# Expert routing on quarters of the array, four output buffers, and a feed-forward pass laid over a butterfly product

## The chip, the core and the metric

The kernel runs on one core of a Trainium2 chip. The core has five engines that are used here: TensorE (PE, matrix products from SBUF into PSUM), VectorE (DVE), ScalarE (ACT), GpSimd (POOL) and SyncE (SP, which here only issues DMA transfers); POOL issues transfers too. Engines order themselves by semaphores: an instruction adds to one when it ends, another engine waits until it has reached a number. Each engine works through its own instructions in the order in which they are written. The metric is the device time of one execution in microseconds (us), the median of several runs.

## The reference

Two layers work on x of 2 x 2048 tokens with 256 features, in float32. Each layer is a mixer (a state space scan) followed by a feed-forward block, with layer norms around them. The change is in the feed-forward block of layer 0 and in the end of layer 1.

Layer 0's block is a mixture of experts with 64 slots. Tokens stand in groups of 16. In each group every slot takes the token with the highest logit:

```python
logits = einsum('...btd,des->...btes', grouped, controller) + tie
perm = (logits == max(logits, axis=-3))
sel = einsum('...btd,...btes->...besd', grouped, perm)
inner = relu(einsum('...besd,desf->...besf', sel, f1) + bias)
inter = einsum('...besf,esfd->...besd', inner, f2)
out = einsum('...besd,...btes->...btd', inter, perm)
```

So there is one 256 x 64 matrix f1 and one 64 x 256 matrix f2 for each of the 64 slots.

The end of layer 1 has two parts that add into one output. The first takes y, the sum of both directions of the mixer: f = relu(W1.y + b1) with 512 hidden features, then y + W2.f + b2, a layer norm over features, and the residual x1 is added. The second takes the normed input xn: a matrix W_exp (256 to 1024), ten butterfly stages over the 1024 features, a bias, gelu, ten more butterfly stages and a matrix W_con back to 256. A butterfly stage mixes each feature with the one whose index differs in one bit, by 2 x 2 weights. The kernel folds the butterfly stages into the two matrices, once, and then multiplies tokens by the folded matrices.

## The kernel before, in words

P is 128, C is 2 (halves of 256 features), TT is 512 tokens, T is 4096 tokens, HB is 8 (blocks of 128 in 1024), FB is 4 (blocks of 128 in 512). `banks` are PSUM tiles of 512 float32 columns; there are eight. A float32 matmul or its weight load appears as two records in the trace, a transpose as one. The name in a trace row is stage_tile: exa is the routing and the expert products, fly the butterflies, fin and finb the last stage.

**experts0.** For each of the two batches, four quarters of 512 tokens are routed, and then eight expert groups (of eight slots) are multiplied. Routing of a quarter: PE computes the logits (line 949) and turns the tokens around with an identity matrix (line 956); DVE adds the tie term, takes the maximum over each group, compares and multiplies by a parity mask (lines 906 to 913), which gives pq; PE transposes pq (line 960); ACT keeps pq in perm_t (862) and the turned tokens in work (864). Two groups of 16 tokens share 32 partitions. To select rows, DVE spreads each transposed 128 x 128 piece into pex, four copies of which three quarters are zero (918, with pair_of as mask), and PE multiplies with all 128 rows and 512 columns (969), eight times a quarter. ACT copies each result into sel_t with the axes turned (870): consecutive elements go to addresses 512 bytes apart. One quarter ends before the next one starts.

For a group of slots, PE forms the first products (979, two column tiles of 64 at a time, `first_products`), DVE adds the bias and applies relu (927, 931), PE forms the second products (993, two row tiles of 64 at a time, `second_products`), and ACT and DVE copy half each into one of two output buffers `inter` (880, 935). POOL stores a buffer (846), waits for the store (850) and then posts slot_free, for which the copies wait. SP loads f1 and f2 of a group into two buffers each (831, 834).

**butterflies and last.** `butterflies` folds ten stages into `up` and `down`, [128, 8, 257] each. Three of them, the cross-block stages, mix whole blocks: ACT scales a block (1906) and DVE adds the scaled partner (1917), eight blocks a stage; then DVE copies the result back (1921). The other seven, the lane stages, mix partitions within a block. For each of 7 x 8 steps and each of the two matrices DVE builds a 128 x 128 matrix with two nonzeros in a row (1950, 1956), PE multiplies a block by it (1973) and ACT copies the result back (1987). `down` gets its cross-block stages first, `up` last. Then the block of instructions ends, and a second one begins. There PE transposes `up` (2064), and for each of eight tiles of 512 tokens it runs hidden (2073), feed (2080), half of upward (2088), mean (2101), the rest of upward, variance (2107) and downward (2112). ACT applies relu, gelu, square, log and exp, DVE the residual (2157), the centring (2163), three Newton instructions (2166 to 2172), scale, shift, x1 and the final sum (2188). The next tile's first matmul waits for the end of the sum. SP loads y and x1 of a tile, POOL stores the output (2053).

## Time and profile before

| | |
|---|---|
| median of 3 runs | 3668.19 us (3656.0 to 3673.11) |
| the profiled execution | 3672.47 us, its span 3670.8 us |
| experts0, routing and products | 680 to 937 us of the span |
| last, both parts | 3181.5 to 3670.8 us of the span |
| PE busy | 2889.5 us (79%) |
| DVE busy | 2834.1 us (77%) |
| ACT busy | 1881.2 us (51%) |
| POOL busy | 2287.1 us (62%) |
| granted TensorE clock, mean | 0.916 |

The span runs from the first to the last instruction of one profiled execution. Busy shares are averages over stages with different limits; the two mixers lie between and before the stages of the change. A granted clock of 1.00 is 2.4 GHz, 0.50 is 1.2 GHz.

### The profile page before, as it was taken

The page shows a single profiled execution, that of the slowest core. Times are in us where ns is not written, and L with a number is a line of the kernel's source. Part 1 is how long each engine was busy: PE and PEld are TensorE (multiplying, and loading weights), DVE is VectorE, ACT ScalarE, POOL GpSimd, SP SyncE. Part 2 cuts the span into 40 slices and gives each one's busy share as a digit, 9 for nine tenths or more (in the row PEclk, how much of TensorE's full clock was granted, in tenths as well). Part 3 has the DMA queues.
Part 4 walks back from the last instruction along what each step waited for, and adds up shares of the span by engine and source line. Part 5 has one row for each costly group of instructions (what it writes and reads, how often), then busy time and mean ns, then how long its engine had stood idle before and what let it go on. Part 6 is the DMA issues. An engine that isn't in the chain of part 4 may idle for free. (4 is left out here: it accounts for less than half of the span.)

```text
span 3670.8 us, 27563 instructions
## 1 busy us (share of the span) xinstructions
PE 2889.5 (79%) x7494; PEld 1196.8 (33%) x7494; DVE 2834.1 (77%) x2237; ACT 1881.2 (51%) x2469; POOL 2287.1 (62%) x1102
## 2 busy tenths in 40 slices
PE   5677677767556879788898888798897887579998
PEld 2222222344222333333333333233333332244443
DVE  4899799433238999999999999999999999462222
ACT  4575576434245555555555655555555554352222
POOL 2598399100116989889889899898899898100000
PEclk7799699899777999999989999999899999889999
DMA  1011011153714444554555455555445555201110
GB/s 58 16 51 47 7 52 50 35 183 114 245 52 153 158 172 172 166 183 168 168 179 172 157 182 177 165 172 174 169 162 181 179 178 200 83 23 34 34 34 11
DMA packets 163606, 451.10 MB, mean 123 GB/s; under 512 B 23328, under 2 KB 52192, under 8 KB 163456
## 3 DMA queue, kind: packets, MB, share of 16 engines
q1 hardware_dynamic: 156576, 424.60, 34.5%
q0 software_dynamic: 6912, 25.17, 1.7%
q8 instruction: 45, 0.74, 0.1%
q14 instruction: 73, 0.60, 0.1%
HBM read 414.85 MB, written 34.87 MB: 123 GB/s over the span
## 5 line engine op out<-in xcount | busy, mean ns | idle before, releaser
L1317 POOL TENSOR_TENSOR mix_prod<-mix_spread,mix_h 128x1024 f32<-128x1024 f32 x512 | 1374.4, 2686 | 247.4 <-DVE mix_h L1723 131.4
L1817 PE MATMUL mix_banks<-mix_prod,kept_ident 128*128 128x512 f32 x2048 | 1049.6, 638 | 80.9 <-POOL mix_prod L1317 54.1
L1367 ACT ACTIVATE mix_side_in<-mix_dt,mix_neg_a 128x1024 f32<-128x1024 f32 x384 | 437.7, 1141 | 315.6 <-DVE mix_h L1723 312.2
L1817 PEld LDWEIGHTS mix_banks<-mix_prod,kept_ident 128*128 128x128 f32 x2048 | 406.1, 202 | 515.8 <-issue 302.9
L1709 DVE TENSOR_TENSOR mix_banks<-mix_banks,mix_dtu 128x1024 f32<-128x1024 f32 x384 | 467.1, 1216 | 10.0 <-PE mix_banks L1807 5.9
L1723 DVE TENSOR_TENSOR_SCAN mix_h<-mix_side_in,mix_state,mix_banks 128x1024 f32<-128x1024 f32 x192 | 450.6, 2347 | 18.1 <-issue 0.4
L1807 PE MATMUL mix_banks<-mix_parts,kept_sel 96*128 96x512 bf16 x768 | 250.0, 410 | 260.5 <-DVE mix_h L1723 252.4
L1723 DVE TENSOR_TENSOR_SCAN mix_h<-mix_side_in,mix_banks 128x1024 f32<-128x1024 f32 x192 | 438.8, 2286 | 18.9 <-ACT mix_side_in L1367 1.3
L1327 POOL TENSOR_TENSOR mix_side_in<-mix_spread,mix_dtu 128x512 f32<-128x512 f32 x256 | 339.0, 1324 | 0.1
L2053 POOL DMA_DIRECT2D out<-finb_o x8 | 5.8, 728 | 525.0 <-DVE finb_eps L2192 525.0
L435 POOL TENSOR_TENSOR mix_drive<-mix_drive,mix_du 128x1024 f32<-128x1024 f32 x128 | 305.2, 2400 | 40.5 <-ACT mix_drive L500 40.3
L638 DVE TENSOR_TENSOR_SCAN mix_h<-mix_banks,mix_state,mix_drive 128x1024 f32<-128x1024 f32 x128 | 296.2, 2339 | 23.7 <-POOL mix_drive L435 21.4
L1359 ACT ACTIVATE mix_state<-mix_h 128x1 f32<-128x1 f32 x256 | 51.7, 202 | 412.4 <-DVE mix_h L1723 411.6
L1807 PEld LDWEIGHTS mix_banks<-mix_parts,kept_sel 96*128 96x128 bf16 x768 | 60.1, 101 | 557.0 <-DVE mix_h L1723 449.4
L1367 ACT ACTIVATE mix_banks<-mix_dt,mix_neg_a 128x1024 f32<-128x1024 f32 x128 | 141.9, 1109 | 121.7 <-DVE mix_h L1723 121.2
L740 PE MATMUL mix_banks<-mix_prod,kept_ident 128*128 128x512 f32 x352 | 178.4, 631 | 10.7 <-DVE mix_u L656 10.7
L846 POOL DMA_DIRECT2D slot_outputs<-exa_inter x32 | 18.3, 573 | 258.1 <-DVE exa_inter L935 181.6
L506 ACT ACTIVATE mix_banks<-mix_dt,mix_neg_a 128x1024 f32<-128x1024 f32 x128 | 141.5, 1105 | 44.4 <-DVE mix_h L638 44.1
L1723 DVE TENSOR_TENSOR_SCAN mix_h<-mix_banks,mix_state,mix_side_in 128x1024 f32<-128x1024 f32 x64 | 149.3, 2333 | 0.0
L1723 DVE TENSOR_TENSOR_SCAN mix_h<-mix_banks,mix_side_in 128x1024 f32<-128x1024 f32 x64 | 145.4, 2272 | 0.0
L500 ACT ACTIVATE mix_drive<-mix_dd,mix_mask 128x1024 f32<-128x1024 f32 x128 | 145.1, 1133 | 0.0
L1579 DVE SCALAR_TENSOR_TENSOR mix_u<-mix_x,mix_taps,mix_u 128x1024 f32<-128x1024 f32 x96 | 122.6, 1279 | 16.1 <-ACT mix_u L1396 15.8
(264 smaller groups left out, 4499.4 us busy)
## 6 DMA issues: line engine op xcount, KB each, us to landing
mix_spread<-c_rows SPq DMA_DIRECT2D x640, 512.0 KB, 3.9
mix_c_row<-c_rows SPq DMA_DIRECT2D x40, 512.0 KB, 3.6
exa_f<-f SPq DMA_DIRECT2D x32, 512.0 KB, 4.8
slot_outputs<-exa_inter POOLq DMA_DIRECT2D x32, 512.0 KB, 3.9
ln_zp<-slot_outputs SPq DMA_DIRECT2D x8, 2048.0 KB, 10.2
first_acc<-xT SPq DMA_DIRECT2D x8, 512.0 KB, 4.1
x_scratch<-first_acc POOLq DMA_DIRECT2D x8, 512.0 KB, 4.0
fw_scratch<-mix_res SPq DMA_DIRECT2D x8, 512.0 KB, 6.3
```

Source lines behind the costliest of these rows:

```text
L435: pool.tensor_tensor(r.drive[:, i % 3, :], r.drive[:, i % 3, :], part(du, i // NS), ALU.add).then_inc(r.drive_ready, 1)
L500: act.activation(r.drive[:, i % 3, :], part(dd, i // NS), ACT.Copy, scale=mask[:, at:at + 1]).then_inc(mask_ready, 1)
L506: act.activation(decay[i % 2], part(dt, i // NS), ACT.Exp, scale=neg_a[:, at:at + 1]).then_inc(r.decay_ready, 1)
L638: dve.tensor_tensor_scan(r.h[:, i % 3, :], decay[i % 2], r.drive[:, i % 3, :], state[:, at:at + 1], ALU.mult, ALU.add).then_inc(r.scan_don ...
L740: mm = pe.matmul(y_bank[:, q, :], which, r.prod[:, i % 2, q * TT:(q + 1) * TT], start=i % NS == 0, stop=True, skip_group_check=True)
L1317: pool.tensor_tensor(prod[:, un % 2, :], spread[:, i % SLOTS, :], h[:, un % HR, :], ALU.mult).then_inc(prod_ready, 1)
L1327: ins = pool.tensor_tensor(half(side_in[:, 2, :], hf), half(spread[:, i % SLOTS, :], hf), half(dtu[:, g % MB, :], hf), ALU.mult)
L1367: act.activation(drive[un % 2] if pooled(un) else side_in[:, un % 2, :], dt[:, at // NS, :], ACT.Exp, scale=neg_a[:, way(p), at:at + 1]).t ...
L1709: dve.tensor_tensor(drive[un % 2], drive[un % 2], dtu[:, at // NS, :], ALU.mult).then_inc(drive_ready, 1)
L1723: dve.tensor_tensor_scan(h[:, un % HR, step], a_in[:, step], b_in[:, step], state[:, at:at + 1] if p % NC else 0.0, ALU.mult, ALU.add).the ...
L1807: mm = pe.matmul(half(drive[un % 2], hf), k.sel[:, at % NS, :], half(parts[:, p % 2, :], hf), start=True, stop=True)
L1817: mm = pe.matmul(y_bank[:, hf, :], k.ident[:], half(prod[:, un % 2, :], hf), start=False, stop=True, skip_group_check=True)
```

## The change

In experts0:

- Selecting no longer uses pex and pair_of. A transposed pq is copied once into pq_t, and for every 128 tokens and each half of the features four matmuls with 32 rows each (partitions 0 to 31, 32 to 63 and so on) and 128 columns are issued, each with its own PSUM bank, 4 to 7. A quarter is done in two halves of two 128-token pieces. ACT copies banks 4 and 5 of a half, DVE banks 6 and 7, each by four instructions of 256 elements.
- The tokens are transposed straight from xn; work has two halves for the turned tokens.
- The logits of the next quarter are issued ahead of the selecting matmuls of this one, and DVE makes the next quarter's choice ahead of its copies.
- There are four output buffers in place of two. ACT and DVE wait for the store itself instead of slot_free. DVE's relu of the next group stands ahead of its copies of this group.
- All loops are written out instead of run by registers.

In last, the two blocks of instructions are one. W1 and y of tile 0 are loaded first. The parts hidden, feed, mean and variance of all eight tiles, with their norm and residual, are run first, results in `base` (all eight tiles stay in SBUF). The lane steps are spread over tiles 1 to 5: each tile has eight places, and SLOT_STEPS says how many steps it gets. Each direction has one PSUM bank in place of two. The results of the cross-block stages are used where they are, without the copy back. Mean, centring, square, variance and root of a tile are done during the next tile, the finish during the one after it. `across(1)` stands on ACT behind tile 0's relus, `across(0)` ahead of tile 7's relus. Then `up` is transposed over two banks, with the rest of tile 7's norm in between, and eight tiles of upward, gelu and downward follow with nothing else than the final sum. SP stores the output.

The core of the diff, its new lines (the old ones stand in the functions above). First experts0: POOL, the copies that two engines share, DVE, selecting, and the order on PE:

```diff
+                for n in range(B * NE):
+                    b, e = n // NE, n % NE
+                    for h in range(2):
+                        r = (2 * n + h) % KEPT
+                        pool.wait_ge(act_kept, 2 * n + h + 1)
+                        pool.wait_ge(dve_kept, 2 * n + h + 1)
+                        pool.dma_start(z[b, :, e * EG + h * 4:e * EG + h * 4 + 4, :], inter[:, r]).then_inc(stored[r], 16)
+                for r in range(KEPT):
+                    pool.wait_ge(stored[r], 16 * (2 * B * NE // KEPT))
+
+            def selected(i, hh, v, c):
+
+                t0 = i % NQ * QG + hh * 16
+                to = sel_t[:, c, :, t0:t0 + 16].rearrange("p s (t g) -> p t g s", t=2)[:, :, 2 * v:2 * v + 2, :]
+                return to, banks[:, 4 + v, :].rearrange("p (t c g s) -> p t c g s", t=2, c=C, g=2)[:, :, c]
...
+                def keep_turned(i):
+                    dve.wait_ge(turned, i + 1)
+                    if i >= 2:
+                        dve.wait_ge(sel_ready, 2 * (i - 1))
+                    dve.tensor_copy(pq_t[:, i % 2].rearrange("p t n -> p (t n)"), banks[:, 3, :]).then_inc(pq_ready, 1)
+
+                def keep_selected(i, hh):
+                    dve.wait_ge(sel_ready, 2 * i + hh + 1)
+                    if i // NQ:
+                        dve.wait_ge(in_ready, i // NQ * NE)
+                    for v in (2, 3):
+                        for c in range(C):
+                            to, of = selected(i, hh, v, c)
+                            ins = dve.tensor_copy(to, of)
+                    ins.then_inc(dve_sel, 1)
...
+                def select(i, hh):
+                    b, j = i // NQ, i % 2
+                    pe.wait_ge(xtok_ready, i + 1)
+                    pe.wait_ge(pq_ready, i + 1)
+                    if i or hh:
+                        pe.wait_ge(act_sel, 2 * i + hh)
+                        pe.wait_ge(dve_sel, 2 * i + hh)
+                    if b and i % NQ == 0 and hh == 0:
+                        pe.wait_ge(inner_ready, b * NE)
+                        pe.wait_ge(act_kept, b * 2 * NE)
+                        pe.wait_ge(dve_kept, b * 2 * NE)
+                    for t in range(2):
+                        for c in range(C):
+                            for v in range(4):
+                                rows = slice(32 * v, 32 * v + 32)
+                                o = (t * C + c) * P
+                                mm = pe.matmul(banks[:, 4 + v, o:o + P], xtok[rows, j, 2 * hh + t, c * P:(c + 1) * P],
+                                               pq_t[rows, j, 2 * hh + t, :], start=True, stop=True)
+                    mm.then_inc(sel_ready, 1)
...
+                for b in range(B):
+                    logits(b * NQ)
+                    turn(b * NQ)
+                    for i in range(b * NQ, (b + 1) * NQ):
+                        ahead = i + 1 < (b + 1) * NQ
+                        if ahead:
+                            logits(i + 1)
+                        for hh in range(2):
+                            select(i, hh)
+                        if ahead:
+                            turn(i + 1)
+                    pe.wait_ge(act_sel, 2 * NQ * (b + 1))
+                    pe.wait_ge(dve_sel, 2 * NQ * (b + 1))
+                    first_products(b * NE)
                     for e in range(NE):
                         if e + 1 < NE:
-                            first_products(e + 1)
-                        second_products(e)
+                            first_products(b * NE + e + 1)
+                        second_products(b * NE + e)
```

Then last: loads, the order on ACT, finish, the order on DVE, the lane steps and the order on PE:

```diff
+            def load_y(i):
+                if i >= 2:
+                    sp.wait_ge(summed, i - 1)
+                sp.dma_start(y[:, i % 2], token_tile(k.y, i, L)).then_inc(y_loaded[i % 2], 16)
+
+            def load_x1(i):
+                if i >= 2:
+                    sp.wait_ge(finished, i - 1)
+                sp.dma_start(x1[:, i % 2], token_tile(k.x1, i, 0)).then_inc(x1_loaded[i % 2], 16)
+
+            sp.dma_start(w1[:], a["W1"].rearrange("(c p) m -> p c m", p=P)).then_inc(w1_loaded, 16)
+            load_y(0)
+            for dst, src in ((b1[:], a["b1"]), (vec[:], a["vec"]), (up_b[:], a["up_bias"])):
+                sp.dma_start(dst, src).then_inc(vec_loaded, 16)
+            sp.dma_start(fac[:], a["factors"]).then_inc(fac_loaded, 16)
+            sp.dma_start(down[:, :, 0:E], a["W_con"].rearrange("(j p) e -> p j e", p=P)).then_inc(down_loaded, 16)
+            sp.dma_start(w2[:], a["W2"].rearrange("(c p) m -> p c m", p=P)).then_inc(w2_loaded, 16)
+            load_y(1)
+            sp.dma_start(up[:], a["exp"].rearrange("(j p) e -> p j e", p=P)).then_inc(up_loaded, 16)
+            load_x1(0)
+            load_x1(1)
...
+            act.preload_act_table_set("natural_log_exp_and_others")
+            act.wait_ge(vec_loaded, 48)
+            act.wait_ge(filled, 1)
+            for i in range(NT):
+                if i == NT - 1:
+                    across(0)
+                at = marks(i)
+                for h in range(FB):
+                    relu(i, h)
+                    lanes(at[h], at[h + 1])
+                if i == 0:
+                    act.wait_ge(fac_loaded, 16)
+                    act.wait_ge(down_loaded, 16)
+                    across(1)
+                lanes(at[4], at[5])
+                if i:
+                    square(i - 1)
+                lanes(at[5], at[7])
+                if i:
+                    root(i - 1)
+                lanes(at[7], at[8])
+            square(NT - 1)
...
+            def finish(i):
+                dve.wait_ge(root_ready, i + 1)
+                dve.scalar_tensor_tensor(out=ra[:], in0=banks[:, 7, :], scalar=EPS, in1=r0[:], op0=ALU.add,
+                                         op1=ALU.mult).then_inc(newton, 1)
+                dve.wait_ge(newton, 5 * i + 1)
+                dve.scalar_tensor_tensor(out=ra[:], in0=ra[:], scalar=-0.5, in1=r0[:], op0=ALU.mult,
+                                         op1=ALU.mult).then_inc(newton, 1)
+                dve.wait_ge(newton, 5 * i + 2)
...
+            for i in range(NT):
+                at = marks(i)
+                lanes(at[0], at[1])
+                if i >= 2:
+                    finish(i - 2)
+                lanes(at[1], at[4])
+                if i:
+                    centre(i - 1)
+                lanes(at[4], at[7])
+                residual(i)
+                lanes(at[7], at[8])
+                if i == NT - 2:
+                    across(0)
+            dve.wait_ge(crossed[0], ACROSS * HB)
+            dve.tensor_tensor(up_b[:], up_b[:], spare[:, :, E:W].rearrange("p j o -> p (j o)"), ALU.add).then_inc(biased, 1)
...
                     for w in range(2):
-                        i = n * (2 * HB) + (2 * j + w)
-                        slot = (2 * j + w) % 4
-                        pe.wait_ge(mat_ready, i + 1)
-                        pe.wait_ge(kept, i + 1)
-                        pe.matmul(banks[:, slot, 0:width], mat[:, slot, :], way[w][0][:, j, :], start=True,
+                        if s == 0:
+                            pe.wait_ge(up_loaded, 16)
+                            pe.wait_ge(crossed[1], ACROSS * HB)
+                        pe.wait_ge(mat_ready, 2 * s + w + 1)
+                        if s:
+                            pe.wait_ge(kept, 2 * (s - 1) + w + 1)
+                        src = spare if w and n == 0 else way[w][0]
+                        pe.matmul(banks[:, w, 0:W], mat[:, (2 * s + w) % 4, :], src[:, j, :], start=True,
                                   stop=True).then_inc(turned, 1)
 
...
+            for i in range(NT):
+                at = marks(i)
+                for h in range(FB):
+                    hidden(i, h)
+                    lanes(at[h], at[h + 1])
+                if i:
+                    mean(i - 1)
+                lanes(at[4], at[5])
+                for c in range(C):
+                    feed(i, c)
+                    lanes(at[5 + c], at[6 + c])
+                if i:
+                    variance(i - 1)
+                lanes(at[7], at[8])
+            pe.wait_ge(crossed[0], ACROSS * HB)
+            for n in range(HB * C):
+                if n >= 2:
+                    pe.wait_ge(w_ready, n - 1)
+                else:
+                    pe.wait_ge(kept, 2 * len(lane_steps))
```

## Rows read from the trace of the kernel before

**Rows 1.** Busy time by stage: stretch, length, busy us of each engine, PEclk, DMA share, GB/s.

```profile
680.00:940.00 260.00, 178.18 (x1024) 100.90 (x1024) 84.28 (x131) 103.02 (x121) 18.33 (x32) 0.87 0.36 130
3181.50:3670.80 489.30, 424.02 (x1072) 199.49 (x1072) 159.56 (x436) 167.58 (x296) 5.83 (x8) 0.95 0.10 33
```

**Rows 2.** The same view inside the experts stage: routing, products, twice, and two groups.

```profile
681.90:753.10 71.20, 55.06 (x128) 21.31 (x128) 21.73 (x32) 42.04 (x44) 0.00 (x0) 0.85 0.08 28
753.10:811.00 57.90, 37.85 (x385) 31.54 (x385) 19.69 (x32) 9.74 (x17) 8.10 (x14) 0.88 0.75 264
811.00:879.40 68.40, 51.50 (x130) 19.79 (x130) 21.73 (x32) 41.45 (x44) 1.06 (x2) 0.90 0.06 22
879.40:937.00 57.60, 33.77 (x384) 28.27 (x384) 19.68 (x32) 9.55 (x16) 9.16 (x16) 0.89 0.70 255
786.00:798.00 12.00, 7.79 (x96) 6.70 (x96) 4.76 (x8) 2.39 (x4) 2.21 (x4) 1.00 0.87 308
```

**Rows 3.** Order of events, one quarter of the routing: start us, duration us, instruction.

```profile
810.89 0.30 PEld L949 LDWEIGHTS exa_banks<-kept_xn,exa_ctrl 128*128 128x128 f32 x2 [2.41 <-issue]
...
815.09 0.69 DVE L913 TENSOR_TENSOR exa_pq<-exa_lt,exa_parity 128x512 f32<-128x512 f32 x1
...
826.50 0.30 PEld L949 LDWEIGHTS exa_banks<-kept_xn,exa_ctrl 128*128 128x128 f32 x2 [0.59 <-issue]
```

**Rows 4.** Groups by form in the experts stage.

```profile
L870 ACT ACTIVATE exa_sel_t<-exa_banks 128x512 f32 x64 | 63.7, 1040 | 28.4 <-PE exa_banks L969 28.3
...
L935 DVE COPY exa_inter<-exa_banks 128x512 f32<-128x512 f32 x32 | 22.1, 691 | 65.6 <-POOLq L850 50.6 <-PE exa_banks L993 15.0
...
L880 ACT ACTIVATE exa_inter<-exa_banks 128x512 f32<-128x512 f32 x32 | 19.1, 597 | 91.2 <-POOLq L850 70.7 <-PE exa_banks L993 20.5
```

**Rows 5.** Busy time by stretch in the last stage; the last is one tile.

```profile
3181.50:3201.70 20.20, 0.00 (x0) 0.00 (x0) 13.27 (x44) 9.92 (x24) 0.00 (x0) 0.50 0.53 165
3201.70:3259.10 57.40, 56.65 (x224) 39.17 (x224) 54.36 (x222) 43.19 (x113) 0.00 (x0) 0.97 0.00 0
3259.10:3282.10 23.00, 3.67 (x16) 2.91 (x16) 14.76 (x44) 9.89 (x24) 0.00 (x0) 0.66 0.18 61
3332.10:3379.80 47.70, 45.17 (x104) 19.55 (x104) 9.65 (x16) 13.07 (x17) 0.75 (x1) 1.00 0.11 33
```

**Rows 6.** Order of events: matmuls on tiles of the array, and the last output copy.

```profile
756.79 2.00 PE L993 MATMUL exa_banks<-exa_f,exa_work 64*128 64x256 f32 x16
...
787.98 1.97 PE L979 MATMUL exa_banks<-exa_sel_t,exa_f 128*64 128x128 f32 x32
...
794.11 1.97 PE L979 MATMUL exa_banks<-exa_sel_t,exa_f 128*64 128x128 f32 x32
...
931.21 0.69 DVE L935 COPY exa_inter<-exa_banks 128x512 f32<-128x512 f32 x1 [0.69 <-POOLq L850]
...
952.78 0.64 PE L1042 MATMUL ln_by_token<-ln_zp,exp_perm_t 128*32 128x256 f32 x8
```

**Rows 7.** Order of events in the last stage.

```profile
3187.95 3.31 ACT L1906 ACTIVATE fina_spare<-fin_down,fina_fac 128x257 f32<-128x257 f32 x8 [18.90 <-DMA fin_down<-W_con]
...
3199.71 1.23 DVE L1921 COPY fin_down<-fina_spare 128x2056 f32<-128x2056 f32 x1
...
3276.64 0.39 SPq L2042 DMA_DIRECT2D finb_y<-both_scratch  x1
...
3282.12 9.47 PE L2073 MATMUL finb_banks<-finb_y,fin_w 128*128 128x512 f32 x16 [6.15 <-DMA finb_x<-x_scratch]
...
3316.51 13.90 PE L2112 MATMUL finb_banks<-finb_g,fin_down 128*128 128x512 f32 x32
...
3332.13 7.13 PE L2073 MATMUL finb_banks<-finb_y,fin_w 128*128 128x512 f32 x16 [1.72 <-DVE finb_eps L2192]
```

**Rows 8.** Groups by form in the last stage.

```profile
L1987 ACT ACTIVATE fin_up<-fly_banks 128x257 f32<-128x257 f32 x56 | 21.6, 386 | 13.5 <-PE fly_banks L1973 7.9
...
L2166 DVE SCALAR_TENSOR_TENSOR finb_ra<-finb_banks,finb_r 128x512 f32<-128x512 f32 x8 | 5.5, 691 | 71.2 <-ACT finb_r L2138 71.2
```

815 lines of the change are left out of this document (384 added, 431 removed).

## The prediction

> **What bounds the kernel now.** I read the busy shares by stage first. The two touched stages hold 260 us (experts) and 489.3 us (last) of the 3670.8 us [rows 1]; nothing between them is edited, so only these count.
>
> The experts stage runs a routing part and a product part for each batch [rows 2]. In routing PE is 77% busy and nothing is full. The order of events shows a strict chain per quarter of 512 tokens: logits from 810.89, DVE's choice until 815.8, two kinds of transposes, then eight selecting matmuls that wait for ACT's copies, and the next logits at 826.50: 15.6 us [rows 3]. ACT pays for the copies: 1040 ns to scatter 512 elements into sel_t, against 597 ns for 512 written in long runs [rows 4]. The products are held by the round output copy, store, slot free: ACT and DVE wait 70.7 and 50.6 us for POOL's slots [rows 4], and the DMA engines are 70 to 87% busy [rows 2].
>
> The last stage has four pieces in a row: 20.2 us of loads and the first cross-block steps, 57.4 us of butterflies, 23.0 us of cross-block steps, transposes and loads, then eight tiles of 47.7 us, in which PE works 45.2 [rows 5]. PE's own work sets nearly all of the tiles.
>
> **The experts, routing.** Removed: ACT's copy of the tokens, pair_of, pex and DVE's four products into it per quarter, and eight full-size matmuls (16 records of 0.43 us, 6.9 us). Added: 32 matmuls of 32 rows and 128 columns (64 records); eight copies of 256 elements on ACT and eight on DVE; one DVE copy of 512 (pq_t).
>
> The new shape of matmul is in no row. Four column tiles took 0.64 us for eight records of 256 columns; two row tiles took 2.00 us for 16 such records, 0.108 us apart after the first; two column tiles of 128 columns took 1.97 us for 32, 0.055 apart [rows 6]. If four row tiles run side by side, a record costs about 0.04 us, 2.6 us a quarter; if each weight load has to follow the last, 0.108 us, 6.9 us, as now. I take 0.04, since tiles overlap in all three rows, and keep 0.108 as the bound. The Trainium skill ("TensorE: Matmul & The Clock Gate", LDWEIGHTS (loading the stationary operand)) speaks against this change: a load goes by columns, 32 rows costing as much as 128; one after another that gives the second value. Its Part 3 has loads of different row groups overlap, which gives the first.
>
> Copies: ACT needs 386 ns for a dense 257 [rows 8] and 597 for 512 [rows 4], a fixed part of 0.17; with it the scattered 1040 gives 0.60 us for a scattered 256, 2.5 us with handover for a half's four. DVE's dense copy of 512 takes 691 ns [rows 4]; its scattered 256 is in no row. Bounds 0.35 (half of it) and 0.60 (ACT's); I take 0.60, the nearest scattered row. The Trainium skill ("SBUF — State Buffer", Door 1: The DMA port swizzle) says that accesses which leave a 16-byte line each time pay; ACT's two rows agree (1040 against 597), and by it DVE pays too.
>
> A quarter then, from the moment turned(i) is posted: DVE copies pq_t while PE does the logits of i+1 (to 1.8), chooses for i+1 (4 x 0.72, to 4.7), copies half 0 (2.4, to 7.2). Only then may PE select half 1, as banks 4 to 7 are single: behind that wait on PE stand the transposes of i+1. Select and latencies 1.5, DVE's copies 2.4, to 11.1, and the next keep_turned follows. DVE's cycle is 0.7 + 2.9 + 2.4 + 1.5 + 2.4 + 0.4 = 10.3 us; ACT's, 9 us, hides behind it. PE is half busy in it, and the granted clock was 0.85 and 0.90 with more [rows 2]; at 1.2 GHz logits and select(1) cost 2.9 more. I take 11. A batch: first logits, choice and transposes 5.6, three quarters 33, the last, with nothing to choose, 9.7: 48.3 us. Before: 71.2 and 68.4 [rows 2]. **Gain 43 us.** Bounds: 9 us a quarter (gain 56), 14 (gain 24).
>
> **The experts, products.** Four output buffers end the slot round, and DVE's relu goes ahead of the copies. What is late next is the DMA: a group moves 1 MB in and 1 MB out, and the engines were 0.87 busy at 308 GB/s [rows 2], so 354 GB/s when full: 5.9 us for 2.1 MB. Undisturbed groups already take 6.1 us (787.98 to 794.11 [rows 6]). PE needs 2.0 + 2.0 us, DVE 2.6. SP issues f1(n+1) behind f2(n), which waits for second_products(n-2): as before. The parts take 57.5 and 52.5 us now to the last copy (931.9 [rows 6]); 6.6 for the first group and 7 x 6.1 make 49.3 after. **Gain 11 us**; bounds 27 (5.0 us a group: PE's 4.0 and its handovers) and a loss of 1 (7.0). Setup: PE waits for the tie load, which lands when the removed memsets end: nothing. Loops written out: no row prices fetching the longer code; taken as nothing, bound 2 us either way.
>
> **Last stage, start.** PE's first matmul is at 3201.76 now [rows 5]. After, W1 and y(0) are first in SP's queue, 1 MB together; two such loads now hold PE from the issue at 3276.64 until 3282.12, 5.5 us [rows 7], so PE starts near 3187. Its first 16 records run cold as at 3282 (9.47 us against 7.13 [rows 7]), relu 0.9, feed 6.9: 3204.1. Factors and W_con come behind the small vectors, in time, for ACT starts across(1) only behind relu(0,3), at 3197.2: 11.7 us (3187.95 to 3199.7 [rows 7]), then residual(0) 1.4 on DVE, then the first matrix: PE resumes at 3211.1, after 5.3 us idle. The two copies of 1.23 us behind the cross-block steps are gone.
>
> **Tiles 1 to 5 over the butterflies.** PE work of a tile: 40 records (16 hidden, 16 feed, 8 mean and variance) of 0.4292 (13.90 us for 32 [rows 7]) are 17.2 us; 11 steps of four records of half that, 9.5: together 26.7. The stalls, walked through in DVE's order:
> - centre(i-1) stands ahead of the matrices that PE wants right behind mean(i-1): 0.2 + 1.3 + 0.7 = 2.25 us.
> - finish(i-2), seven instructions x 0.72 = 5.0 [rows 8], stands ahead of slot 1: 0.6; residual 1.4 ahead of slot 7, with ACT's root between its two copies: 0.9.
> - one bank per direction: the second step of a slot waits for ACT's 0.39 us copy [rows 8]: 0.3 to 0.5, three times, 1.2.
> That is 31.6 us a tile. Tile 1 (no finish, 12 steps) ends at 3236.3, tile 5 at 3362.7, the steps behind it at 3368.3.
>
> **Tiles 6 and 7, transition.** Tile 6: 17.2, to 3385.5. In tile 7 across(0) stands ahead of all relus on ACT and begins behind root(5): 1.6 + 11.2 + 0.7, PE idle 10.1 us and then cold (3.4 us more); variance(6) ends at 3416.3. Transposes go over two banks instead of four, 0.33 us each instead of 0.22 (3.67 us for 16 [rows 5]), with finish(6) (1.6 + 5.0), mean(7) 1.7, centre(7) 1.3 and variance(7) 1.7 in line: 16.7 us and 2.3 cold: 3435.3.
>
> **Final tiles.** 64 records x 0.4292 = 27.5 us x 8 = 219.8: 3655.1; two additions 1.3 and a store from SP 4.2: 3660.6 against 3670.8. So the eight tiles shrink by 162 us, and the part ahead of them grows from 100.6 to 253.8 us, by 153: PE does the same matmuls. **Gain 10; I take 8**, since PE may be cold behind the 5.3 us too. Bounds: all stalls of the tiles gone (25 us) and tile 7's wait halved, gain 38; twice the stalls, loss 17.
>
> **Sum.** 43 + 11 + 8 = 62 us. The profiled execution took 3672.5 (span 3670.8), so 3610.5; the median 3668.2 lies 4.3 lower, so **3606 us**.
>
> **Rivals.**
> - *Row tiles do not overlap.* Each half's select takes 3.4 us instead of 1.3; both lie mostly on the cycle, with more cold clock: 14 us a quarter, gain 24, sum 43: 3625. For it: the overlapping rows have 64 rows or narrow weights; against: they all overlap. 0.17.
> - *The last stage hides its stalls:* gain 38 there: 3576. For it: DVE has only 18 us of work in a 31.6 us tile. 0.15.
> - *The four buffers do nothing,* as the DMA keeps the products at their time: 3617. 0.12.
> - *The other side: PE falls to 1.2 GHz in the interleaved part.* 137 + 48 = 185 us of PE work lie between 3187 and 3435 and double when cold; once 43% of it is cold (80 us = 62 + 18) the kernel is slower by over 0.5%; all of it: 3791. Against: gaps of 1.7 us between today's tiles leave the clock at 1.00, and the butterflies run at 0.97 [rows 5, 7]. 0.04.
> - The forecast: 0.52.
>
> **How the numbers follow.** The range goes from the well hidden last stage with a little more from the routing (3570) to the serial row tiles with a loss in the last stage (3640). Under 0.5% (18 us) a change of this kernel can't be told from none. Faster takes all cases but the cold one and the far end of the bounds: 0.92; same 0.04; slower 0.04.
>
> **What would show it.** Right: selecting records some 0.04 us apart; 10 to 12 us between logits; no waits for POOL, and DMA share near 0.9 in the products; PE's first matmul of the last stage 5.5 us behind its first load; about 31 us a tile, with PE waiting for matrices behind mean; 27.5 us a final tile. Wrong: weight loads of 0.1 us in a row; scattered DVE copies far from 0.6 us; PEclk under 0.9 in the interleaved part; a wait in tile 7 that isn't 10 us.

## The result and the profile after

The changed kernel takes 3600.8 us (median of 4 runs, 3594.44 to 3601.67) against 3667.24 (median of 4, 3656.0 to 3673.11): a ratio of 0.9826, 95% interval 0.9804 to 0.9848, so 56 to 72 us less. The forecast was 3606 us, 62 us less by its sum. The profiled execution took 3600.97 us, with a span of 3599.2.

First the stretches of the changed kernel, in the view of busy time by stretch (its columns are those of [rows 2] and [rows 5]): routing, products, routing, products; the whole last stage; and in it the start, tiles 1 to 5, tile 6 with the wait of tile 7, the rest of tile 7 with the transposes, and the eight final tiles.

```profile
680.50:730.60 50.10, 31.16 (x320) 22.21 (x321) 28.65 (x52) 21.20 (x40) 0.00 (x0) 0.77 0.11 37
730.60:781.30 50.70, 38.03 (x384) 32.09 (x385) 19.58 (x32) 9.56 (x16) 8.20 (x15) 0.84 0.78 280
781.30:829.50 48.20, 30.23 (x320) 22.18 (x320) 28.65 (x52) 21.21 (x40) 0.53 (x1) 0.78 0.14 56
829.50:878.30 48.80, 36.53 (x384) 30.92 (x384) 19.46 (x33) 9.58 (x17) 7.98 (x15) 0.88 0.76 271
3121.20:3599.20 478.00, 428.66 (x1072) 204.31 (x1072) 149.26 (x411) 145.16 (x282) 0.00 (x0) 0.96 0.10 34
3126.70:3150.70 24.00, 18.36 (x37) 7.66 (x37) 12.24 (x32) 13.13 (x29) 0.00 (x0) 0.86 0.49 169
3150.70:3312.90 162.20, 144.84 (x421) 80.07 (x422) 87.10 (x272) 62.90 (x145) 0.00 (x0) 0.96 0.09 30
3312.90:3343.00 30.10, 20.60 (x48) 8.77 (x47) 15.91 (x34) 15.90 (x34) 0.00 (x0) 0.89 0.10 35
3343.00:3374.90 31.90, 25.05 (x57) 11.14 (x58) 17.32 (x37) 5.38 (x7) 0.00 (x0) 0.84 0.05 17
3374.90:3594.70 219.80, 219.80 (x513) 96.68 (x511) 13.84 (x21) 46.57 (x67) 0.00 (x0) 1.00 0.05 17
```

Set against [rows 2] the reader sees where the time went: routing took 71.2 and 68.4 us and takes 50.1 and 48.2; the products went from 57.9 and 52.5 (to the last copy, [rows 6]) to 50.7 and 48.8. From the first logits to the last output copy that is 250.0 us before and 197.8 after: 52.2 less. The first logits come 1.4 us earlier. The last stage took 489.2 us from its first load to the end of the span and takes 477.8, 11.4 less. Both stages differ by some us between profiles of one program; how much is said with the first and the second experiment. These make 65.0 of the 71.6 us between the two spans. The other 6.6 lie between the last output copy and the last stage, where no line is changed; run before_again below says what they are.

One quarter of the new routing, in the order of events (start us, duration us, instruction, and in brackets the idle time ahead of it and what ended it):

```profile
788.72 0.69 DVE L922 COPY exa_pq_t<-exa_banks 128x512 f32<-128x512 f32 x1 [0.75 <-PE exa_banks L996]
...
790.33 1.17 PE L1015 MATMUL exa_banks<-exa_pq_t,exa_work 32*128 32x128 f32 x32
790.44 0.69 DVE L905 TENSOR_TENSOR exa_lt<-exa_banks,exa_tie 128x512 f32<-128x512 f32 x1 [1.03 <-PE exa_banks L978]
...
793.22 1.86 DVE L931 COPY exa_sel_t<-exa_banks 128x256 f32<-128x256 f32 x4
...
795.23 2.09 PE L1015 MATMUL exa_banks<-exa_pq_t,exa_work 32*128 32x128 f32 x32 [3.73 <-DVE exa_sel_t L931]
...
797.38 1.92 DVE L931 COPY exa_sel_t<-exa_banks 128x256 f32<-128x256 f32 x4 [2.29 <-PE exa_banks L1015]
...
800.11 0.69 DVE L922 COPY exa_pq_t<-exa_banks 128x512 f32<-128x512 f32 x1 [0.81 <-PE exa_banks L996]
```

The 32 records of one selecting half take 1.17 us at 2.4 GHz, 0.037 us apart, and 2.09 at 1.2 GHz. From one copy of pq_t to the next go 11.4 us: DVE works for 7.2 of them and waits 4.1 for PE. PE in turn waits 3.73 us for DVE between the two halves, because the whole choice for the next quarter stands ahead of DVE's copies; behind that wait it runs at 1.2 GHz.

The groups by form of the same stage:

```profile
L1027 PE MATMUL exa_banks<-exa_sel_t,exa_f 128*64 128x128 f32 x512 | 42.3, 337 | 24.0 <-DMA exa_f<-f 20.0 <-ACT exa_sel_t L869 4.1
...
L869 ACT ACTIVATE exa_sel_t<-exa_banks 128x256 f32<-128x256 f32 x64 | 30.7, 630 | 41.1 <-PE exa_banks L1015 41.1
L931 DVE COPY exa_sel_t<-exa_banks 128x256 f32<-128x256 f32 x64 | 30.2, 585 | 20.1 <-PE exa_banks L1015 20.1
...
L952 DVE COPY exa_inter<-exa_banks 128x512 f32<-128x512 f32 x32 | 22.1, 690 | 8.2 <-PE exa_banks L1042 4.1 <-DMA slot_outputs<-exa_inter 4.0
```

A scattered copy of 256 elements takes 630 ns on ACT and 585 on DVE. The output copies wait 4.0 us in all for a store, where they waited 50.6 and more for POOL [rows 4]; PE's wait is now the load of f1, 20.0 us.

In the last stage, one tile over the butterflies, and the wait in tile 7:

```profile
3228.94 1.88 PE L2231 MATMUL fin_banks<-fin_base,kept_mean 128*128 128x512 f32 x4
3230.86 1.28 DVE L2130 TENSOR_TENSOR fin_base<-fin_base,fin_banks 128x512 f32<-128x512 f32 x2 [4.87 <-PE fin_banks L2231]
...
3232.85 0.70 PE L2253 MATMUL fin_banks<-fin_up,fin_mat 128*128 128x257 f32 x2 [2.03 <-DVE fin_mat L2114]
...
3249.05 0.67 PE L2253 MATMUL fin_banks<-fin_up,fin_mat 128*128 128x257 f32 x2 [0.94 <-DVE fin_mat L2114]
...
3343.05 2.93 PE L2211 MATMUL fin_banks<-fin_y,fin_w 128*128 128x512 f32 x3 [9.55 <-ACT fin_f L2043]
```

DVE's centring (1.28 us) stands between mean and the next matrices, and PE waits 2.03 us for them. Behind that wait feed's first eight records run partly at 1.2 GHz in this tile and in tile 1 (5.29 and 5.02 us, where others take 3.60):

```profile
3202.45 3.60 PE L2222 MATMUL fin_banks<-fin_f,fin_w 128*128 128x512 f32 x8
...
3233.82 5.29 PE L2222 MATMUL fin_banks<-fin_f,fin_w 128*128 128x512 f32 x8
```

The first is tile 2, the second tile 3. At the end of each tile PE waits another 0.94 us, and in tile 7 9.55 us for the relu behind across(0). From one tile's first hidden record to the next it is 31.4, 33.1, 31.4 and 31.4 us for tiles 2 to 5. Tile 1 takes 33.0 from the second of its four hidden products on; the first stands ahead of the butterflies.

### The profile page after: what moved, and what is told of

Same layout as the page of the kernel before. It is cut to its first block and busy times, and to the rows that moved or that the text cites. A ratio compares the mean times of both kernels' runs of the same rounds, so it can differ in the third digit from the quotient of the medians.

```text
span 3599.2 us, 26475 instructions
## 1 busy us (share of the span) xinstructions
PE 2852.6 (79%) x7878; PEld 1208.1 (34%) x7878; DVE 2831.8 (79%) x2234; ACT 1817.9 (51%) x2447; POOL 2280.4 (63%) x1094
## 5 line engine op out<-in xcount | busy, mean ns | idle before, releaser
L435 POOL TENSOR_TENSOR mix_drive<-mix_drive,mix_du 128x1024 f32<-128x1024 f32 x128 | 305.2, 2400 | 41.2 <-ACT mix_drive L500 40.8
L2199 DVE TENSOR_TENSOR fin_base<-fin_banks,fin_base 128x512 f32<-128x512 f32 x16 | 10.3, 686 | 204.4 <-PE fin_banks L2271 204.4
L838 POOL DMA_DIRECT2D slot_outputs<-exa_inter x32 | 17.2, 539 | 205.7 <-DVE exa_inter L952 201.3
```

The source lines that it names most:

```text
L435: pool.tensor_tensor(r.drive[:, i % 3, :], r.drive[:, i % 3, :], part(du, i // NS), ALU.add).then_inc(r.drive_ready, 1)
```

## The experiments

Times are medians; a ratio is that to the kernel before, run beside it on the same chip, with its interval. Stage times are from each run's own profile. "The changed kernel" has 197.8 us in the experts stage (from the start of the first logits to the end of the last output copy; the expectations have 197.9) and 224.1 from the first butterfly matmul (3150.69) to the first upward matmul (3374.79). The interval of the changed kernel (0.9804 to 0.9848) overlaps those of all the kernels below that try to improve on it, except all_tuned; what each of them gains is read from stage times, of one profile each.

### Each half alone: experts_only, last_only

```diff
 # experts_only: kernel before, with
-def experts0 of before
+def experts0 of the changed kernel
 # last_only: changed kernel, with experts0 of before
```

> The kernel before with the new experts stage alone; the last stage is the old one. My theory: the two halves of the change do not touch each other, so the experts stage keeps its 197.8 us from the first logits to the last output copy (250.0 before) and the last stage its 489 us. That is 52 us, a time near 3615. The changed kernel's profile also has 6.3 us less inside the unedited second mixer (first to last POOL product there 2006.7 us against 2013.0) and 1.4 us less ahead of the first logits. Theory A: the 6.3 us are a difference between two executions, so this run shows a mixer anywhere between 2005 and 2015 us, unrelated to the edit. Theory B: they come from the new experts stage (its code or its buffers move what follows), so the mixer takes 2007 us here and 2013 us in the run with the last stage alone.

> The changed kernel with the experts stage of before, so the new last stage alone. My theory: the last stage takes 478 us against 489.2, a gain of 11, a time near 3656. The rival that says the last stage is worth nothing gives 3667, and that it hides its stalls 3629. The tiles must show the same pieces as in the changed kernel: 24.0 us from the first matmul to the first butterfly matmul, some 32 us a tile, 9.6 us of wait in tile 7, 27.5 us a final tile. For the mixer between the stages: 2013 us if theory B of the run beside this one holds, any value from 2005 to 2015 if theory A does.

experts_only: 3606.45 us, ratio 0.9853 (0.9831 to 0.9875), 46 to 62 us. Its experts stage takes 197.8 us. last_only: 3655.48 us, ratio 0.9977 (0.9964 to 0.9989), 4 to 13 us. Its pieces are those of the changed kernel: 23.8 us to the first butterfly matmul, 163.8 for tiles 1 to 5, 9.6 of wait in tile 7. So the halves add up, and each is worth about what was forecast (54 and 8). The old experts stage takes 256.5 us in last_only's profile and 250.0 in the first one: the old stage itself varies, the new one stays within 0.5 us in the six profiles that hold it unchanged.

The new last stage varies too. Six profiles hold it unchanged: in three (the changed kernel, two_buffers, split_choice) it takes 477.7 to 477.8 us from its first load to the end, in three (last_only, rows_in_turn, three_loads) 482.8 to 483.0; from the first butterfly to the first upward matmul that is 224.0 to 224.1 and 228.6. The waits are the same, and the 4.5 us are records at 1.2 GHz: 1.6 in tiles 1 to 5, 2.9 behind them. The clearest is variance(7), in the changed kernel and in rows_in_turn:

```profile
3373.06 1.89 PE L2239 MATMUL fin_banks<-fin_sq,kept_mean 128*128 128x512 f32 x4
```

```profile
3404.96 3.62 PE L2239 MATMUL fin_banks<-fin_sq,kept_mean 128*128 128x512 f32 x4
```

The old last stage took 489.1 to 489.8 us in its three profiles, so the new one gains 6 to 12 us and not 11.4 each time, which fits last_only's 4 to 13. The second mixer took 2003.6 us in experts_only and 2013.0 in last_only; that alone would fit theory B.

### The mixer that nobody edited: before_again

> The kernel before, profiled once more. The unedited second mixer took 2013.0 us from its first to its last POOL product in both profiles with the old experts stage, and 1996.3 to 2007.0 in eight with the new one; the granted clock in it was 0.94 in the long ones and 0.96 in the two of 1996.3. If its length is set by the execution and its clock, this profile may show any value in 1996 to 2015; if the new experts stage shortens it, 2013 again.

The mixer from its first to its last POOL product, by stretch: before, before_again, and a kernel with the new experts stage (two_buffers):

```profile
1114.10:3127.10 2013.00, 1685.29 (x3904) 669.63 (x3904) 1947.39 (x1196) 1128.91 (x1469) 1766.58 (x826) 0.94 0.51 172
```

```profile
1114.40:3113.90 1999.50, 1669.84 (x3904) 664.23 (x3904) 1939.52 (x1196) 1129.29 (x1469) 1761.85 (x826) 0.95 0.51 174
```

```profile
1068.50:3064.80 1996.30, 1658.65 (x3904) 660.42 (x3904) 1938.48 (x1196) 1128.94 (x1469) 1760.73 (x826) 0.96 0.51 174
```

The same program needs 13.5 us less in the same stretch in another execution. Theory B falls: the 6.3 us in the mixer are within what executions differ by. The granted clock goes with it: 0.94 in five of the six profiles of 2006.7 to 2013.0 (0.95 in three_loads), 0.96 in the two of 1996.3; which drives which isn't shown. The old experts stage took 253.7 us here, so its three profiles average 253.4 and the new stage is worth 55.5 us rather than 52.2.

### Do the row tiles overlap: rows_in_turn

```diff
-                    for t in range(2):
-                        for c in range(C):
-                            for v in range(4):
+                    for v in range(4):
+                        for t in range(2):
+                            for c in range(C):
```

> The changed kernel with the loop over the four row groups outside: four matmuls of one row group follow each other, then the next group's. Work, copies and buffers are the same. My theory: neighbours in the order overlap only because they lie on different row groups, so 32 selecting records take 3.4 us (0.108 apart) in place of 1.2 at full clock; 2.2 us more a half, both on the cycle, 4.4 a quarter and 35 us in all, down to 18 if only one of the halves is on it: 3619 to 3636. The rival: matmuls so short overlap in any order, the records stay 0.03 to 0.04 us apart and the time stays at 3601.

3634.5 us, ratio 0.9925 (0.9907 to 0.9942). The experts stage takes 232.1 us, 34.2 more. A quarter in the order of events:

```profile
704.40 2.82 PE L1015 MATMUL exa_banks<-exa_pq_t,exa_work 32*128 32x128 f32 x32
...
709.39 4.82 PE L1015 MATMUL exa_banks<-exa_pq_t,exa_work 32*128 32x128 f32 x32 [2.17 <-DVE exa_sel_t L931]
...
714.25 1.91 DVE L931 COPY exa_sel_t<-exa_banks 128x256 f32<-128x256 f32 x4 [5.10 <-PE exa_banks L1015]
```

The same 32 records take 2.82 us at full clock, 0.088 apart, where neighbours lie on one row group. So the 0.037 of the changed kernel is overlap between neighbours in the program. Neighbours on different row groups also write to different PSUM banks, since each group has a bank of its own, and no run parts the two; against the bank as the cause stand the first products, which follow each other 0.055 us apart in one bank [rows 6]. The total came out at the top of the expectation although one half costs only 1.65 us more: the second half runs at 1.2 GHz and takes 4.82 where it took 2.09. The Trainium skill ("TensorE: Matmul & The Clock Gate", Part 3) has the rule that a weight load overlaps matmuls in flight only when its row group differs; both kernels agree with it, and here the loop order decided whether the overlap came.

### What the four buffers bring: two_buffers

```diff
-    KEPT = 4
+    KEPT = 2
```

> The changed kernel with KEPT = 2, all else the same. If the transfers alone hold the products (the rival of the prediction that the four buffers do nothing), the products stay at 50.7 and 48.8 us and the time at 3601. If the slot round comes back, ACT and DVE wait for the store of the group before (7.2 us to landing), a group goes from 6.65 to 7 or 7.5 us and the products to 54 to 58 us: 3608 to 3617. Between them I expect the smaller loss, 3606, since the relu stays ahead of the copies and a store has most of a group to land.

3601.67 us, ratio 0.9836 (0.9814 to 0.9858). The experts stage takes 205.9 us, 8.1 more, but the median can't be told from the changed kernel's, and the profile has a mixer 10.4 us shorter. The copies wait again:

```profile
L1042 PE MATMUL exa_banks<-exa_f,exa_work 64*128 64x256 f32 x256 | 36.4, 414 | 10.2 <-DVE exa_inter L952 10.0
...
L952 DVE COPY exa_inter<-exa_banks 128x512 f32<-128x512 f32 x32 | 22.1, 692 | 52.1 <-DMA slot_outputs<-exa_inter 50.4 <-PE exa_banks L1042 1.7
```

DVE's wait for stores is 50.4 us, as long as that for POOL's slots was [rows 4], and yet it costs only 8: PE waits 10.0 us for these copies, and in return only 12.8 in place of 20.0 for f1. The rival that four buffers do nothing falls by the stage time; by the median alone it could not be told.

### What holds the products now: three_loads

```diff
+                def load_f1(n):
+                    if n >= 3:
+                        sp.wait_ge(in_ready, n - 2)
+                    sp.dma_start(f1[:, n % 3], first[:, :, n % NE]).then_inc(f1_loaded[n % 3], 16)
...
-                    if n >= 2:
-                        sp.wait_ge(in_ready, n - 1)
-                    sp.dma_start(f1[:, j], first[:, :, e]).then_inc(f1_loaded[j], 16)
+                    if n + 1 < B * NE:
+                        load_f1(n + 1)
```

> The changed kernel with three buffers for f1 in place of two, and f1 of group n+1 issued ahead of f2 of group n. In the changed kernel a group starts every 6.65 us (738.50 to 771.75, five groups) and PE waits 20 us for exa_f, with the DMA engines 0.78 busy at 280 GB/s. Theory A, that of the prediction: bandwidth holds the products. Then an earlier issue only lengthens the landing, a group stays at 6.1 to 6.6 us and the products at 49 to 50 us: 3598 to 3601. Theory B: the round first_products, f1 free, load landed, holds them; then a group falls towards PE's 5.0 us, the products to 40 to 43 us each and the time to 3585. I take A, since full engines would move a group's 2.1 MB in 5.9 us.

3590.02 us, ratio 0.9787 (0.9751 to 0.9823); the experts stage 188.7 us, 9.1 less, the products 46.4 and 43.6 us. The starts of first_products (they follow at 6.65 us in the changed kernel):

```profile
738.16 1.97 PE L1032 MATMUL exa_banks<-exa_sel_t,exa_f 128*64 128x128 f32 x32
741.98 1.97 PE L1032 MATMUL exa_banks<-exa_sel_t,exa_f 128*64 128x128 f32 x32
745.81 1.97 PE L1032 MATMUL exa_banks<-exa_sel_t,exa_f 128*64 128x128 f32 x32
753.44 2.97 PE L1032 MATMUL exa_banks<-exa_sel_t,exa_f 128*64 128x128 f32 x32
758.27 1.97 PE L1032 MATMUL exa_banks<-exa_sel_t,exa_f 128*64 128x128 f32 x32
763.82 1.97 PE L1032 MATMUL exa_banks<-exa_sel_t,exa_f 128*64 128x128 f32 x32
```

Neither theory holds alone. Two groups start at PE's own pace of 3.8 us, on what has been loaded ahead; the next three take 7.6, 4.8 and 5.6 us, 6.0 on average (745.81 to 763.82). The view of busy time by stretch for these 18 us, and for five steady groups of the changed kernel:

```profile
745.81:763.82 18.01, 13.23 (x146) 10.81 (x144) 8.05 (x13) 4.18 (x7) 3.34 (x6) 0.91 1.05 403
```

```profile
738.50:771.70 33.20, 24.26 (x242) 20.09 (x240) 12.93 (x21) 6.57 (x11) 6.07 (x11) 0.85 0.87 317
```

In three_loads the DMA engines are full there (a share of 1.05, so the transfers do hold these groups) and move 403 GB/s, 7.3 MB in 18 us, more than three groups' 6.3. So the prediction's estimate of 354 GB/s for full engines was too low: at 403 a group's 2.1 MB need 5.2 us and not 5.9. In the changed kernel the engines reach 0.87 and 317 GB/s, and what three_loads gains is the time that they lost to loads issued late. PE's wait has moved from f1 (20.0 us) to f2 (16.7 us), whose load now stands behind f1's.

### The order of DVE in the routing: split_choice

```diff
                         keep_turned(i)
-                        if i + 1 < (b + 1) * NQ:
-                            choose(i + 1)
-                        for hh in range(2):
-                            keep_selected(i, hh)
+                        if ahead:
+                            best(i + 1)
+                        keep_selected(i, 0)
+                        if ahead:
+                            mark(i + 1)
+                        keep_selected(i, 1)
```

`best` is the sum and the maximum of `choose`, `mark` its comparison and product.

> The changed kernel with DVE's choice for the next quarter cut in two: sum and maximum, then the copies of half 0, then comparison and product, then the copies of half 1. In the changed kernel PE waits 3.73 us for DVE's copies between the two selecting halves, since the whole choice (2.9 us) stands ahead of them, and the second half then runs at 1.2 GHz (2.09 us against 1.17). My theory: a quarter is DVE's cycle, and the cut lets half of the choice run while PE selects half 1. A quarter falls from 11.0 to some 9 us, six such quarters give 10 to 14 us, routing takes 43 us a batch in place of 50.1 and 48.2. Rival: the cycle is as long in any order, for DVE's work stays the same (the transposes of pq wait for the product, now later), and a quarter stays at 10.5 to 11 us: gain under 3 us.

3589.5 us, ratio 0.9798 (0.9758 to 0.9838); the experts stage 186.6 us, 11.2 less, routing 45.3 and 41.2 us. The logits are 10.6 and 9.2 us apart in the first batch, 7.7 and 9.0 in the second. DVE's work is the same, only its place:

```profile
793.72 1.88 DVE L934 COPY exa_sel_t<-exa_banks 128x256 f32<-128x256 f32 x4
795.45 0.67 DVE L912 TENSOR_TENSOR exa_lt<-exa_lt,exa_top 128x512 f32<-128x512 f32 x1
795.86 1.17 PE L1022 MATMUL exa_banks<-exa_pq_t,exa_work 32*128 32x128 f32 x32 [2.21 <-ACT exa_sel_t L869]
...
797.09 1.92 DVE L934 COPY exa_sel_t<-exa_banks 128x256 f32<-128x256 f32 x4 [0.25 <-PE exa_banks L1022]
```

PE waits 2.21 in place of 3.73 us and stays at 2.4 GHz (1.17 us in place of 2.09), and DVE waits 0.25 for it in place of 2.29: 1.5 us of wait and 0.9 of clock. The quarter's length was not set by DVE's work alone; it was a chain that alternates between two engines.

### The stalls of the last stage: centre_later, all_later, spread_cross, last_tuned

```diff
 # centre_later, DVE, tile i
-                if i:
-                    centre(i - 1)
-                lanes(at[4], at[7])
+                lanes(at[4], at[5])
+                if i:
+                    centre(i - 1)
+                lanes(at[5], at[7])
 # all_later: finish(i - 2) behind lanes(at[0], at[2]), residual(i) behind lanes(at[5], at[8]) too
 # spread_cross, ACT (DVE has the same halves ahead of its centre)
-                if i == NT - 1:
-                    across(0)
                 for h in range(FB):
                     relu(i, h)
+                    if i == NT - 2:
+                        part(h)
+                    if i == NT - 1 and h < 2:
+                        part(4 + h)
 # last_tuned: both, and on ACT root(i - 1) behind lanes(at[7], at[8])
```

> The changed kernel with DVE's centre(i-1) behind the matrices of the place after mean(i-1) instead of ahead of them. PE waits 2.03 us there in each of tiles 1 to 5 (3230.8 to 3232.85). My theory: the wait is only DVE's order, so it goes five times, tiles 1 to 5 take 152 us instead of 162 (3150.7 to 3312.9), and the time falls by 8 to 10 us. Rival: what is won there comes back as a wait for square or for the next matrices, and the tiles stay at 162. By the clock, PE with fewer gaps may also lose the cold feed of tiles 1, 3 and 5 (5.13 us against 3.43): 5 us more.

> The changed kernel with DVE's finish(i-2), centre(i-1) and residual(i) each one place later than now, behind the matrices that PE wants next. PE's waits for matrices are 18.7 us in all, for ACT's copies 2.6. My theory: nearly all of the 18.7 go, tiles 1 to 5 take 145 to 150 us, and the time falls by 12 to 17 us against the changed kernel. Rival, two matrices ahead are too few: finish takes 5 us and the two steps ahead cover 3, so a wait of 2 us a tile stays and the gain is 8.

> The changed kernel with across(0) cut into six halves of a step, four placed behind the relus of tile 6 and two behind the first two relus of tile 7, on ACT and DVE alike. PE's wait of 9.55 us in tile 7 and the cold 2.0 us behind it should go. Given back: each half is 1.65 us of ACT between two relus, where hidden takes 1.72 and relu 0.69, so 0.6 us each, 3.7 in all. My theory: tiles 6 and 7 take 7 to 8 us less. Rival: DVE is late instead, since finish(4) and finish(5), 5 us each, stand ahead of its halves, so the next step's ACT half waits and the relus behind it with it; the wait moves and the gain is under 3 us.

> The last stage with all the orders together: finish, centre and residual a place later, across(0) in halves over tiles 6 and 7, and ACT's root(i-1) behind the last copies of the tile, since a wait of 1.7 us a tile was left at its end in all_later (0.94 of it at the first step of the last place) behind root. The experts stage is that of the changed kernel. My theory: from the first butterfly matmul to the first upward matmul 224.1 us in the changed kernel, 15.0 less by centre, 1.3 by the others, 8.7 by the halves and 8 by root: 191 us, the time 33 us under the changed kernel's. Rival: root was not the releaser that counts there, and the 1.7 us a tile stay: 199 us.

centre_later: 3587.27 us, ratio 0.9779 (0.9744 to 0.9814). Tiles 1 to 5:

```profile
3151.00:3298.20 147.20, 140.02 (x421) 79.11 (x422) 87.88 (x272) 63.46 (x145) 0.00 (x0) 0.98 0.10 33
```

15.0 us less than in the changed kernel. The view of PE's waits over these tiles (instruction, what it waited for, us in all, times, longest), of the changed kernel, centre_later and last_tuned:

```profile
PE fin_banks L2253 <- DVE fin_mat L2114: 18.7, 10, 4.8
PE fin_banks L2253 <- ACT fin_up L2037: 2.6, 7, 0.9
```

```profile
PE fin_banks L2254 <- DVE fin_mat L2114: 8.6, 5, 4.8
```

```profile
PE fin_banks L2276 <- DVE fin_mat L2124: 6.6, 5, 4.8
PE fin_banks L2276 <- ACT fin_up L2046: 0.6, 2, 0.3
```

Ten waits make 18.7 us: one of 4.8, the first matrix behind across(1); five of 2.03 behind centre; four of 0.94 at a tile's end. centre_later takes the five, 10.1 us, and with them the two feeds at 1.2 GHz, 1.6 and 1.7 us; 0.3 us a tile more I can't put to a wait. It confirms the theory for the tiles, with the clock's part as well. To the first upward matmul it is 211.8 us, 12.3 less: the part behind the tiles takes 64.7 us where the changed kernel's profile has 62.0, within what the unchanged stage shows (62.0 or 65.0).

all_later: 3585.63 us, ratio 0.9782 (0.9746 to 0.9818), tiles 1 to 5 in 145.9 us. The waits are those of centre_later, 8.6 and 2.6 us. My 12 to 17 us came (16.3) although the step that I gave for them was wrong: moving finish and residual bought 1.3 us, and to the first upward matmul it is 209.9 us, 14.2 less. I had read 18.7 us as waits within the tiles, and had divided the 8.6 that stayed by five, 1.7 us a tile, when 4.8 of it is the start and 0.94 a tile is left. So last_tuned's 191 us couldn't come: 3579.14 us, ratio 0.9771 (0.9731 to 0.9811), 199.5 us in place of 224.1, and tiles 1 to 5 in 144.1. Root was the releaser at the tile's end, for behind the last copies it takes the 0.94 to 0.45 and ACT's 2.6 to 0.6, but that was little to win, and it cost more in tile 6, where PE now waits for the last relu ahead of feed:

```profile
3307.49 6.28 PE L2245 MATMUL fin_banks<-fin_f,fin_w 128*128 128x512 f32 x14 [3.57 <-ACT fin_f L2052]
```

In spread_cross this wait is 0.52 us. With root later DVE waits 3.34 us for it ahead of finish(4), its halves of the cross-block steps start later, ACT waits 3.04 us for them, and the relu stands behind ACT's next half. That is the rival of spread_cross (DVE is late), and it comes true here.

spread_cross: 3592.86 us, ratio 0.9798 (0.9762 to 0.9834); 215.4 us in place of 224.1, 8.7 less. No hidden record of tile 6 or 7 waits; one wait of feed for a relu (0.52 us) makes tile 6 0.8 us longer, of the 3.7 that I had it give back. Another 1.7 us went to the clock: variance(7), behind the transposes, runs at 1.2 GHz (3.4 us) where the changed kernel's profile has it at 2.4 (1.7); since half the profiles of the unchanged stage have it cold too, this isn't shown to come from the edit. The rival falls here; DVE isn't late.

### All together: all_tuned

> split_choice, three_loads and last_tuned in one kernel. Each alone took, against the changed kernel's profile, 11.3 us and 9.2 us from the experts stage (197.9) and 24.6 us from the last (224.1 between the first butterfly and the first upward matmul). They touch different waits, so I expect the sum, 45 us: experts 177 us, the last stage's piece 199.5, the time near 3556. Rival: the shorter routing leaves the products with loads that have had less time to land, and the two gains in the experts stage overlap by up to 5 us.

3553.34 us (3544.88 to 3560.14, 5 runs), ratio 0.9678 (0.9661 to 0.9695) to the kernel before. The experts stage takes 177.9 us, as expected; from the first butterfly to the first upward matmul it is 202.8, 3.3 more than in last_tuned, with tiles 1 to 5 as there (144.3). Tile 6 has last_tuned's wait again (3.58 us), and feed behind it takes 9.77 us where it took 7.13 there: 2.6 of the 3.3. This is the fastest of the kernels tried, and the only one of these whose interval lies clear of the changed kernel's.

## Why the prediction came true, point by point

**Routing, 43 us forecast, 41.3 measured** (139.6 to 98.3). The record of 0.04 us was right (0.037), and rows_in_turn shows that overlap between neighbours on different row groups (and banks) is the reason. The rival of serial row tiles falls: it had 3.4 us a half, and 1.17 was measured. The second batch took 7.4 us to the first transposes of pq, 33.0 for three quarters and 7.9 for the last, 48.3 in all, where I had 5.6, 33 and 9.7. The single steps are less exact than that sum. A half's four scattered copies take 1.9 us and not 2.4, 1.0 less a quarter; against it stand matmuls at 1.2 GHz, 2.09 us for the second half, and DVE's waits for the logits and the transposes, 1.03 and 0.81. That the sum fits so closely is in part luck. I had called the 11 us DVE's cycle; DVE works for 7.2 of them, and split_choice, which shortens it without less work, shows that it is the order of the handovers.

**Products, 11 us forecast, 10.9 measured** (7.2 and 3.7). A steady group takes 6.65 us and not 6.1; the first and the last groups, with no loads to wait for, are quicker. That the two errors cancel is luck, and so is the reference: the two other profiles of the old stage have 111.4 and 113.5 us in the products where the first has 110.4, and 142.3 and 143.0 in the routing where it has 139.6. No waits for POOL are left, as forecast, and the DMA engines are 0.87 busy in the steady groups, near the 0.9 that I gave, and 0.78 over the whole part. The rival that four buffers do nothing falls by two_buffers' stage time, 8.1 of the 10.9. The step that was wrong is the rate of the transfers: the engines moved 403 GB/s when full (three_loads) and not 354, so a group could take 5.2 us, and the transfers hold it at 6.65 only together with the late issue of f1.

**Last stage, 8 us forecast (10 worked out), 11.4 measured in this profile, 6 to 12 over all.** PE starts 5.3 us behind the first load (5.5); its first 16 records take 9.50 us (9.47); the first matrix is multiplied 24.0 us behind that (24.1). Tiles 1 to 5 take 162.2 us where I had 157.2, and the mis-sized term is the clock: two feeds cost 3.3 us more, and the first butterflies and hidden records 2.4 (1.84 us for four, where later ones take 0.87, and 3.33 for 1.88). The prediction's way there has a slip: the end of tile 1, 3236.3, leaves out the idle 5.3 us, and 5.6 us of steps behind tile 5 make up for it, though all 56 steps lie inside tiles 1 to 5; its own terms give 3367.6 where it has 3368.3. A tile without cold records is 31.4 (31.6): the wait behind centre 2.03 (2.25), at the end 0.94 (0.9), none for finish (0.6), the rest in short gaps. Tile 6 takes 17.2 (17.2). In tile 7 PE waits 9.55 us (10.1) and runs cold for 2.0 (3.4). From the end of variance(6) to the first final tile it is 16.0 (19.0). The eight final tiles are 219.8, to the tenth, and the tail 4.5 (5.5). The rival that the stalls are hidden falls, since they cost 10.1 and 3.3 us by centre_later alone. So does the other side: the interleaved part has a granted clock of 0.96, not under 0.9.

**Setup, nothing forecast, 1.4 us measured** in one pair of profiles. With the old setup the first logits came at 680.5 in last_only and at 679.8 in before_again, so it isn't shown to be the edit. What the written-out loops cost, taken as nothing, no run separates.

**The sum.** 62 us were forecast. In the profiles the two stages gave 63.6 and the setup 1.4; 6.6 of the 71.6 lie in unedited code. Against the medians it is 66.4, and the interval leaves 56 to 72.

## What to carry to other kernels

A small matmul on a quarter of the array pays only if its neighbours in the program sit on other quarters: the order of three loops was worth 34 us here. Where two engines hand work to and fro, look at what stands ahead of the handover on each of them, not at either one's busy time; cutting one block of work in two, or moving 1.3 us of it behind the next handover, gave 11 and 15 us. And before a sum of waits is divided by the number of tiles, look at the longest of them: here it was no tile's.

## What the runs showed of the hardware

- Selecting records of 32 rows and 128 float32 columns follow each other 0.037 us apart on alternating row groups, 0.088 apart on the same one (1.17 and 2.82 us for 32). Each row group wrote a PSUM bank of its own, so the two orders differ in the banks of neighbours too.
- Scattered writes with a stride of 512 bytes cost DVE as well: 585 ns for 256 elements, where 512 dense ones take 691 [rows 4]; on ACT 630 and 597. The Trainium skill ("SBUF — State Buffer", Door 1: The DMA port swizzle) has accesses that leave a 16-byte line each time pay; the rows agree for both engines (half of DVE's 691 would be 346, an estimate). Four in a row take 1.86 to 1.92 us, so they start some 0.43 apart.
- Behind the same wait of 2.03 us with the same work around it, PE fell to 1.2 GHz in tiles 1 and 3 and not in 2, 4 and 5; in last_only and rows_in_turn it fell in tile 5 too.
- The DMA engines moved 403 GB/s over 18 us at a share of 1.05 (three_loads, 745.81 to 763.82), and 317 GB/s at 0.87 in the changed kernel's products.
- The same program's second mixer took 1999.5 and 2013.0 us in two executions, at granted clocks of 0.95 and 0.94.
